# Last walk of a two-layer graph network: where the opening and closing products stand, and which engine scales the dense rows

## What is computed

```python
def _L0_gnn_ref(x, edge_index, edge_attr, Wf, bf, Wq, Wk, Wa, Wu, bu):
    ...
    s = numerator / denominator
    z = s * f
    aggr = jax.ops.segment_sum(z, src, num_segments=N_NODES)
    return (x + aggr) @ Wu + bu
def _L1_gnn_ref(h, e, src, dst):
    ...
    def f(y):
        return jax.ops.segment_sum(y[src3] * e3, dst3, num_segments=N)
    k1 = f(x)
    k2 = f(x + dt * k1 / 3)
    k3 = f(x + dt * (k2 - k1 / 3))
    k4 = f(x + dt * (k1 - k2 + k3))
    y = x + dt * 0.125 * (k1 + 3 * (k2 + k3) + k4)
x = _layernorm(x + _L0_gnn_ref(x, edge_index, edge_attr_70, ...), axis=-1)
x = _layernorm(x + _L1_gnn_ref(x, edge_attr3_4x1, src, dst), axis=-1)
```

## Time and profile before

| | us |
|---|---|
| median of 3 runs | 3495.58 |
| the three runs | 3494.34 to 3498.09 |
| the profiled execution, its own time | 3501.67 |
| its span, first to last instruction | 3499.9 |

### The profile page before, as it was taken

The page is one execution under the profiler, slowest core; times in us unless marked ns, Lnnn a source line. Parts: engine busy times, 40 slices in busy tenths (PEclk is TensorE's granted clock), DMA queues, the critical chain, the costliest instruction groups (busy, mean ns, idle before and its releaser), DMA issues.

```text
span 3499.9 us, 31921 instructions
## 1 busy us (share of the span) xinstructions
PE 1189.6 (34%) x6041; PEld 999.4 (29%) x6041; DVE 2478.0 (71%) x6241; ACT 1452.2 (41%) x3372; POOL 2597.1 (74%) x2761
## 2 busy tenths in 40 slices
PE   4666664666661311101111101111100000047777
PEld 4555653544441211101111101111000000046776
DVE  7677616888888786657777767777769999943332
ACT  4445544666661222213333323333325555533333
POOL 7777766777757777767777767777767777748888
PEclk8777787788875555555555555555555555568888
DMA  5555585666653444436777767777757777777775
GB/s 134 172 167 176 175 174 159 217 211 213 215 193 114 147 138 151 147 121 220 252 255 241 248 202 243 247 253 254 237 180 261 263 260 259 264 215 196 197 205 142
DMA packets 423033, 710.22 MB, mean 203 GB/s; under 512 B 100050, under 2 KB 286734, under 8 KB 416592
## 3 DMA queue, kind: packets, MB, share of 16 engines
q1 hardware_dynamic: 235754, 474.50, 40.0%
q0 software_dynamic: 82128, 182.11, 19.2%
q10 hardware_dynamic: 104960, 51.58, 5.1%
HBM read 370.71 MB, written 337.25 MB: 202 GB/s over the span
## 4 chain that ended last, share of the span: by engine, by line
POOL 43%; issue 17%; DVE 14%; PE 8%; DMA 2%; ACT 2%; ACTq 0%; DVEq 0%; SPq 0%; POOLq 0%
POOL gs L1573 32%; POOL gs L834 10%; PE psum L1937 8%; DVE psum L1689 3%; DVE stats L1239 2%; DVE tn L1654 2%; DVE da L1699 2%; DVE psum L1670 2%; DVE new_res L1233 2%; ACT psum L1632 1%; DVE mv L1245 1%; DMA gs<-u,far_row 0%; PE psum L1919 0%; DVE last_z L1695 0%; DMA u<-cross,first_idx 0%
## 5 line engine op out<-in xcount | busy, mean ns | idle before, releaser
L1573 POOL DMA_INDIRECT gs<-u,far_row x1176 | 1115.4, 948 | 363.6 <-issue 357.4
L1133 PE MATMUL psum<-wu_i,d_xt 128*128 128x128 f32 (+1 forms) x782 | 210.9, 443 | 1100.0 <-DVE d_res L1165 1099.9
L1632 ACT ACTIVATE psum<-da 128x512 f32<-128x512 f32 x288 | 173.1, 601 | 888.3 <-DVE tn L1654 553.8
L1670 DVE TENSOR_TENSOR psum<-gs,psum 128x1024 f32<-128x1024 f32 x192 | 234.9, 1224 | 419.0 <-DMA gs<-u,far_row 285.1
L1133 PEld LDWEIGHTS psum<-wu_i,d_xt 128*128 128x128 f32 (+1 forms) x782 | 176.4, 326 | 1136.4 <-issue 1136.4
L343 POOL DMA_INDIRECT pt<-in_x_dram,idx x392 | 386.1, 985 | 123.6 <-issue 119.0
L834 POOL DMA_INDIRECT gs<-rows_e,edge_id x392 | 370.9, 946 | 141.4 <-issue 119.1
L1573 POOL DMA_INDIRECT gs<-x1s,far_row x392 | 374.2, 955 | 120.7 <-issue 119.1
L1689 DVE TENSOR_TENSOR_SCAN psum<-goes_on,psum 128x1024 f32<-128x1024 f32 (+1 forms) x200 | 447.5, 2238 | 0.6
L1909 DVE TENSOR_TENSOR hot<-pos,rel_s 128x1536 f32<-128x1536 f32 x66 | 125.4, 1903 | 255.3 <-ACT psum L1975 228.1
L1937 PE MATMUL psum<-ring,hot 128*128 x1584 | 292.4, 340 | 11.0 <-issue 1.6
(11 more groups left out here) (286 smaller groups left out, 3944.4 us busy)
## 6 DMA issues: line engine op xcount, KB each, us to landing
u<-da SPq DMA_DIRECT2D x144, 512.0 KB, 4.0
rows_e<-pt SPq DMA_DIRECT2D x48, 1056.0 KB, 4.7
total<-tn SPq DMA_DIRECT2D x98, 512.0 KB, 3.3
gs<-total SPq DMA_DIRECT2D x98, 512.0 KB, 5.9
fin_d<-normed SPq DMA_DIRECT2D x49, 516.0 KB, 4.9
ring<-fin_d SPq DMA_DIRECT2D x49, 516.0 KB, 4.7
gs<-u SPq DMA_DIRECT2D x49, 512.0 KB, 5.4
gs<-x1s SPq DMA_DIRECT2D x49, 512.0 KB, 6.4
```

Of the source, the lines that this page charges most:

```text
L1133: t = pe.matmul(d_new_psum[k % 2][0:P, r * D:(r + 1) * D], d_xt[k % 4][:, r * 128:r * 128 + P], wu_i[:, :], start=True, stop=True)
L1573: g.indirect_dma_start(gx[b % 4][:, j * D:(j + 1) * D], None, source[:, :], bass.IndirectOffsetOnAxis(ap=far_row[:, c:c + 1], axis=0)).the ...
L1632: act.mul(shared, half(us[b % 3], i), share).then_inc(shared_set, 1)
L1670: return v.tensor_tensor(zf.rearrange("p (h f) j -> p j h f", h=H), by_head(gxv(b % 4)[:, c0:c1, 0:D]), per_head(wt_rest[:, c0:c1, :] if b ...
```

## The change

It has five parts.

1. On PE, the opening product of the next triple stands between the second and the third product of a triple, and the closing product of the triple before stands behind the first. At the start of a load of 32 words the opening stays in front, and the last triple of a group is closed right behind it.
2. Since two windows can now be open at once, consecutive triples use two spare places (even and odd), the windows turn through 6 banks instead of 7, and `need_b` is the last window of a group less 4 instead of less 6.
3. ACT makes `rest` (with a tile `one` as bias) and multiplies the first 128 of the 384 columns of `nodes` by it, both between setting the bank to zero and the store; POOL multiplies the other 256 and adds the sums to all 384.
4. The table needs five more small DVE operations in hop 0 (in two batches, `ROWB + 4` and `ROWB + 5`).
5. In hop 3, `o_shifts` of the last batch but one stands between the scan and `keep_last`, and no longer between `o_rows` and `o_statistics` of the last batch.

```diff
-SCRATCH = 7 * SLOT
+BANKS = 6
+SCRATCH = BANKS * SLOT
...
-                v.scalar_tensor_tensor(at_open, last_of[1], -float(SCRATCH), moved, ALU.add, ALU.mult).then_inc(walk_set, 1)
-                v.memset(at_close, SCRATCH + SPARE).then_inc(walk_set, 1)
...
+                for odd in range(2):
+                    v.scalar_tensor_tensor(every_other(at_open)[odd], every_other(last_of[1])[odd], -float(SCRATCH + odd * SLOT),
+                                           every_other(moved)[odd], ALU.add, ALU.mult).then_inc(walk_set, 1)
+                    v.tensor_copy(every_other(at_close)[odd][:, 0:1], every_other(moved)[odd][:, 0:1]).then_inc(walk_set, 1)
...
-                next_op(at + 29, need_b, by_group[1], -6.0, ALU.add, 0.0, ALU.max)
+                next_op(at + 34, need_b, by_group[1], -4.0, ALU.add, 0.0, ALU.max)
...
                 add_up_runs(i + 1)
+                if h == 3:
+                    o_shifts(v, b - 1)
                 keep_last(i + 1)
...
                     o_rows(v, b)
-                    o_shifts(v, b - 1)
                     o_statistics(v, b)
...
+                v.memset(one[:, :], 1.0).then_inc(has_none, 1)
...
                     for tri in range(WORDS // 3):
                         g = n * 2 + tri // TRI_OF
                         if tri % TRI_OF == 0:
                             pe.wait_ge(oh_set, base + g + 1)
-                        at = word[WORDS + tri]
-                        open_bank(bass.ds((at >> FIELD).with_bounds(min_val=0, max_val=SCRATCH + SPARE), 2))
+                        if tri == 0:
+                            open_bank(opens(word, tri))
                         for k in range(3 * tri, 3 * tri + 3):
                             pe.matmul(psum[:, bass.ds((word[k] >> FIELD).with_bounds(min_val=0, max_val=SCRATCH - D - 1), D + 1)],
                                       hot[g % OHS][:, k % GROUP, :],
                                       ring[:, bass.ds(word[k] & ((1 << FIELD) - 1), D + 1)], start=False, stop=False)
-                        close_bank(bass.ds((at & ((1 << FIELD) - 1)).with_bounds(min_val=0, max_val=SCRATCH + SPARE), 2))
-                last = (WIN3 - 1) % 7 * SLOT + SPARE
+                            if k % 3 == 0 and tri % TRI_OF > 0:
+                                close_bank(closes(word, tri - 1))
+                            if k % 3 == 1 and tri + 1 < WORDS // 3:
+                                open_bank(opens(word, tri + 1))
+                        if tri % TRI_OF == TRI_OF - 1:
+                            close_bank(closes(word, tri))
+                last = (WIN3 - 1) % BANKS * SLOT + SPARE
...
-                        at, w = m % 7 * SLOT, w_shape(m)[1] * (D + 1)
+                        at, w = m % BANKS * SLOT, w_shape(m)[1] * (D + 1)
                         act.copy(sums_of[m % 4][:, :, :].rearrange("p w f -> p (w f)")[:, 0:w], psum[:, at:at + w]).then_inc(taken, 1)
                         act.wait_ge(taken, taken0 + m + 1)
                         act.copy(psum[:, at:at + WIDE], no_sum[:, 0:1].to_broadcast([128, WIDE])).then_inc(evicted, 1)
+                        if m >= 2:
+                            act.wait_ge(blended, base + m - 1)
+                        n = w_shape(m)[1]
+                        act.activation(rest[m % 2][:, 0:n], sums_of[m % 4][:, 0:n, D], ACT.Identity, bias=one[:, 0:1],
+                                       scale=-1.0).then_inc(rest_set, 1)
+                        act.wait_ge(rest_set, rest_set0 + m + 1)
+                        act.wait_ge(rows_of[m % DNS], rows_of0[m % DNS] + m // DNS * 32 + 16)
+                        P = w_shape(m)[0]
+                        act.activation(nodes[m % DNS][0:P, 0, :], nodes[m % DNS][0:P, 0, :], ACT.Identity,
+                                       scale=rest[m % 2][0:P, 0:1]).then_inc(scaled, 1)
...
-                    g.wait_ge(evicted, base + m + 1)
-                    g.tensor_scalar(rest[m % 2][:, 0:w], t[:, 0:w, D], -1.0, 1.0, ALU.mult, ALU.add).then_inc(has_set, 1)
+                    g.wait_ge(rest_set, rest_set0 + m + 1)
                     g.wait_ge(rows_of[i], rows_of0[i] + m // DNS * 32 + 16)
-                    g.wait_ge(has_set, base + 2 * m + 1)
-                    g.tensor_tensor(nodes[i][0:P, 0:w, :], nodes[i][0:P, 0:w, :],
-                                    rest[m % 2][0:P, 0:w].unsqueeze(2).to_broadcast([P, w, D]), ALU.mult).then_inc(has_set, 1)
-                    g.wait_ge(has_set, base + 2 * m + 2)
+                    if w > 1:
+                        g.tensor_tensor(nodes[i][0:P, 1:w, :], nodes[i][0:P, 1:w, :],
+                                        rest[m % 2][0:P, 1:w].unsqueeze(2).to_broadcast([P, w - 1, D]), ALU.mult
+                                        ).then_inc(has_set, 1)
+                        g.wait_ge(has_set, base + m + 1)
+                    g.wait_ge(scaled, scaled0 + m + 1)
```

More of the change, by code:

```diff
@@ L1398, in places_vector, with every_other @@
             at += 13
+            def every_other(t):
+                return [t.rearrange("o (i k) -> o i k", k=2)[:, :, odd] for odd in range(2)]
             by_group = [t.rearrange("o (g k) -> o g k", k=GROUP)[:, :, GROUP - 1] for t in (block_at[0:1, :], third)]
@@ L1418, in places_vector @@
             if b == ROWB + 3:
-                next_op(at + 10, place, third, 9363.0, ALU.mult)
+                next_op(at + 10, place, third, 10923.0, ALU.mult)
                 next_op(at + 11, place, place, 16, SHR)
                 so_far(at + 12)
-                v.scalar_tensor_tensor(place, place, -7.0, third, ALU.mult, ALU.add).then_inc(walk_set, 1)
+                v.scalar_tensor_tensor(place, place, -float(BANKS), third, ALU.mult, ALU.add).then_inc(walk_set, 1)
             if b == ROWB + 4:
@@ new lines, in places_vector @@
+                so_far(at + 20)
+                v.scalar_tensor_tensor(every_other(at_close)[0][:, 1:TRIS // 2], every_other(last_of[1])[1][:, 0:TRIS // 2 - 1],
+                                       -float(SCRATCH), every_other(moved)[0][:, 1:TRIS // 2], ALU.add, ALU.mult
+                                       ).then_inc(walk_set, 1)
+                v.scalar_tensor_tensor(every_other(at_close)[1], every_other(last_of[1])[0], -float(SCRATCH + SLOT),
+                                       every_other(moved)[1], ALU.add, ALU.mult).then_inc(walk_set, 1)
@@ new lines, in places_vector @@
+            if b == ROWB + 5:
+                for odd in range(2):
+                    next_op(at + 22, every_other(at_open)[odd], every_other(at_open)[odd],
+                            float(SCRATCH + odd * SLOT + SPARE), ALU.add)
+                    next_op(at + 22, every_other(at_close)[odd], every_other(at_close)[odd],
+                            float(SCRATCH + odd * SLOT + SPARE), ALU.add)
+                next_op(at + 26, at_open, at_open, FIELD, ALU.logical_shift_left)
+                so_far(at + 27)
@@ L1441, in places_vector @@
                 v.tensor_tensor(at_open, at_open, at_close, ALU.bitwise_or).then_inc(walk_set, 1)
-                so_far(at + 23)
+                so_far(at + 28)
                 v.tensor_tensor(place, place, window, ALU.add).then_inc(walk_set, 1)
             if b == ROWB + 6:
-                next_op(at + 24, place, place, FIELD, ALU.logical_shift_left)
-                so_far(at + 25)
+                next_op(at + 29, place, place, FIELD, ALU.logical_shift_left)
+                so_far(at + 30)
@@ L1454, in build @@
+                next_op(at + 32, need_a, need_a, 3, SHR)
+                next_op(at + 33, need_a, need_a, float(1 + base), ALU.add)
+                next_op(at + 34, need_b, by_group[1], -4.0, ALU.add, 0.0, ALU.max)
+                next_op(at + 35, need_b, need_b, float(base), ALU.add)
         PIECES = [(b, 0, B) for b in range(NB - 1)] + [(NB - 1, 0, B // 2), (NB - 1, B // 2, B)]
@@ L1843, in build @@
         has_none, has_none0 = idx_zero, 1
+        rest_set, rest_set0 = o_rstd, NB
+        scaled, scaled0 = o_log, NB
         table_in = walk_in
@@ L1854, in build @@
         no_sum = sb("no_sum", [128, 1])
+        one = sb("one", [128, 1])
         def w_shape(m):
```

24 lines of the change are left out of this document (9 added, 15 removed).

## The result

| | before | changed |
|---|---|---|
| median, us | 3494.96 (4 runs, 3494.3 to 3498.09) | 3519.76 (4 runs, 3518.04 to 3529.66) |
| profiled execution, its span | 3501.67, 3499.9 | 3529.66, 3527.2 |

The changed kernel is slower by 24.8 us: ratio 1.0076, 95% interval 1.0063 to 1.0089. The profiled executions differ by 28.0 us; the changed kernel's profiled one is the longest of its four.

What follows compares the result with a forecast made beforehand. PE's sequencer was taken to bound the walk at 3.02 us per window. ACT's delayed issues gave +22 us, all other terms 0; on the median of 3495.58 that made 3517.6, given as 3517, range 3492 to 3534.

Steps and rivals of the forecast that it cites:

- The bound before: Walk from about 3100 us: PE's sequencer, working through its instruction list, sets the pace, 3.02 us per window.
- ScalarE's two operations, +22 us: ACT in the walk: multiplication waiting for `rest` delays the store's issue 0.70 us per window; 3.19 us windows, +22 us.
- Own steps: ACT's work per window of the walk, counted from the first copy: from 2.33 to 3.03 us, against PE's 3.02.
- The rule on the sequencer: Skill's Sequencer Loop: instructions wait for semaphores in the engine's queue, later ones are read meanwhile; DMA issues not late, sum 0.
- Rival (a): ACT in the walk: the delay is hidden or ACT isn't held up; 3496 us, 3490 to 3502; chance 0.17.
- The order of the small products, 0: PE's triples in the walk: same instructions in new order, sequencer's sum unchanged at 396 us; 0.
- rival (b): PE's triples: new order removes the gap before each; 3454 us, with half of it 3475; chance 0.10.
- Six banks and `need_b`, 0: Walk: a `hot` waits two windows more, 6 us out of 11.5 us of cover; 0 by itself.
- GpSimd, 0: POOL in the walk: loses `rest` and a third of a multiplication, but is hardly on the chain; 0 gained.
- Table and hop's end, 0: Hop 0's added table operations: 0, at worst +0.3 us; moved `o_shifts` at the hop's end: 0, within 0.3.
- (c): ACT costs more: every load waits 0.31 us per window, or `rest` takes longer; 43 us, 3539; chance 0.11.
- the main case: ACT's delayed issues slow the walk: +8 to +35 us, 3504 to 3531 us; chance 0.62.

Runs made afterwards that it cites:

- The last run: All of the change but ScalarE's part, with the small products back in their old places, against the kernel before: 3495.06 us, ratio 0.9998.

## Why the prediction was right, point by point

**The bound before.** Sequencer's work sets PE's pace: right, and now shown from three sides. Products alone cost 0, register work costs 0.3 us per triple, and taking register work out gains 18 us until GpSimd stops it, 36 with GpSimd relieved. One reading was loose: "no other engine has more than 2%" of the chain, and 1.1% for GpSimd, hold for single lines; GpSimd's three lines together have more than 2.2%. Nothing hangs on it.

**ScalarE's two operations, +22 us.** Right in kind, place and size: +24.8 for the change, +28 for this part alone. The steps: multiplication at 1.21 us expected, 1.26 measured (the factor took 0.294 us, not 0.281, and began 0.93 us after the first copy, not 0.90). Own steps 3.03 expected; about half of the changed kernel's rounds (60 of 126) take 3.05 to 3.10, so 3.08. What is waited for besides, 0.16 taken; 0.13 measured, since the mean round is 3.21. I had written that ScalarE had 0.69 us to spare; it had 0.39, the rest was already used by loads that wait for a landed store (0.28). The sum held because it doesn't use the 0.69, but charges such waits in the 0.16. That the own steps came out 0.05 longer and the waits 0.03 shorter is luck in the size, not in the mechanism.

**The rule on the sequencer.** Rival (a) was the time that the Trainium skill's Sequencer Loop (Advanced Engine Details and Errata) would give as the prediction reads it: an engine's instruction is put into a queue and waits for its semaphore there. That a DMA issue behind it goes ahead meanwhile is the prediction's reading; the section doesn't say so of DMA issues. The trace does not agree with that reading, for ScalarE: with one wait added the store's issue moved by 0.74 us in the median and the kernel by 29 us. An instruction whose wait is over is passed: the issue at 3210.59 runs beside the copy that began at 3210.58.

**The order of the small products, 0.** Here a step was off. "A sum does not change with its order" holds for the sequencer: its steps have the same length in both kernels. It does not hold for the products themselves, which take 0.2 us more per triple at 1.2 GHz and 0.08 at 2.4. I had set the loss's bound by closings that come later and never asked whether the engine would do the products as fast in another order, though the row at 0.81 us was for the old order alone. By itself it costs 6 us (by which path is open, as said above). In the changed kernel it adds nothing that can be seen, since ScalarE's part alone loses as much as the whole change. The gain that rival (b) hoped for has the wrong sign.

**Six banks and `need_b`, 0.** Right: 3496.53 against 3496.85, and with 11.5 us of cover 6 could go.

**GpSimd, 0.** Right at this pace (3495.46); at PE's faster pace the same relief was worth 18 us.

**Table and hop's end, 0.** The last run holds both, at ratio 0.9998. `o_shifts` stands between the scan and `keep_last` now:

```profile
3076.84 1.23 DVE L1701 TENSOR_TENSOR_SCAN psum<-goes_on,psum 128x512 f32<-128x512 f32 x1
3077.98 0.15 DVE L1223 TENSOR_TENSOR rstd<-rstd,keep 128x8 f32<-128x8 f32 x1
3078.16 0.17 DVE L1225 SCALAR_TENSOR_TENSOR shift<-mv,rstd 128x8 f32<-128x8 f32 x1
3078.25 0.28 DVE L1707 COPY last_z<-psum 128x128 f32<-128x128 f32 x1
```

From the scan to the last statistics it is 3081.28 - 3076.84 = 4.44 us, before 3081.85 - 3077.40 = 4.45.

**Rivals and chances.** (a) and (b) did not happen. (c), 0.31 us of waits in every window, did not either: as I had said for the main case, longer rounds leave fewer loads late, 21 of 126 against 40.

## What to carry to other kernels

An engine's busy share says little about its room: ScalarE was busy 16 of 50 us and had 0.39 us per window to give, since it also issues DMAs and loads registers, in order. Put an operation that waits for its neighbour's result behind the issues and register loads of the same round, not ahead of them; the same work then costs nothing. And where the profile puts PE's idle time down to "issue", as here, count register instructions too, not only products; relieving GpSimd paid only after that.

## What the runs showed of the hardware

- On ScalarE an instruction whose semaphore wait is open holds back the DMA issues and the register load behind it: the store came 1.27 us after the first copy with such a wait and 0.52 without. One without an open wait is passed. One such wait per window moved the issues by 0.74 us and cost 29 us.
- On PE, 264 small products without register instructions of their own cost 0 us, and with them 78 us. A load of 32 words into registers takes 2.43 us in the median of the kernel before, and PE's next register instruction starts 0.06 us after its end; one word takes ScalarE 0.27 to 0.92 us.
- Two small bf16 products side by side between f32 products are cheaper than one here and one there: 1.52 against 1.72 us per triple at 1.2 GHz, 0.81 against 0.89 at 2.4.
- On PE, the register work of an f32 product takes 0.255 us with a mask and a shift in its two addresses, and 0.138 with each address a word of its own.
